# A mixture-of-experts layer that computes, for each token, only the two experts it chose

## The reference

```
scores = sigmoid(xf @ Wg.T + bg + bias)                 # 8 experts
top_scores, top_idx = top_k(scores, 2)
weights = zeros(T, 8).at[arange(T), top_idx].add(top_scores)
h  = gelu(einsum('td,ehd->teh', xf, W1) + b1)           # hidden width 512
eo = einsum('teh,edh->ted', h, W2) + b2
combined = einsum('ted,te->td', eo, weights)            # 6 of 8 weights are zero
shared = gelu(xf @ Ws1.T + bs1) @ Ws2.T + bs2
x = x + shared + combined
```

## Time and profile before

| | |
|---|---|
| median of 3 runs | 1903.09 us |
| the profiled execution's span, first to last instruction | 1898.6 us |
| the difference, what lies around the span | 4.5 us |
| the expert layer, first `up` to last `down` | 155.7 to 656.6 us |
| busy share of the span: PE, DVE, ACT, POOL | 91%, 55%, 71%, 13% |
| mean granted TensorE clock | 0.979 |

### The profile page before, as it was taken

The page is one execution under the profiler, slowest core; times in us unless marked ns, Lnnn a source line. Parts: engine busy times, 40 slices in busy tenths (PEclk is TensorE's granted clock), DMA queues, the critical chain, the costliest instruction groups (busy, mean ns, idle before and its releaser), DMA issues.

```text
span 1898.6 us, 47095 instructions
## 1 busy us (share of the span) xinstructions
PE 1727.9 (91%) x19832; PEld 1120.0 (59%) x19832; DVE 1041.5 (55%) x2670; ACT 1346.8 (71%) x1589; POOL 240.9 (13%) x160
## 2 busy tenths in 40 slices
PE   3458999999999989999999999999988899999998
PEld 2347999999997745555555555555544455555554
DVE  6985212222224445555555555555547777777773
ACT  0454444444443489999999999999998577677765
POOL 6454000000000200000000000000000112211122
PEclk9768999999999999999999999999999999999999
DMA  8001000000000333333333333333230000000000
GB/s 290 1 1 48 1 1 1 1 1 1 1 1 1 65 85 84 86 86 85 86 82 84 84 84 84 80 83 79 58 104 4 1 7 6 6 6 1 7 7 12
DMA packets 36213, 85.68 MB, mean 45 GB/s; under 512 B 10649, under 2 KB 23330, under 8 KB 35618
## 3 DMA queue, kind: packets, MB, share of 16 engines
q1 hardware_dynamic: 33954, 76.30, 17.0%
q0 software_dynamic: 2048, 6.36, 1.1%
HBM read 30.43 MB, written 2.10 MB: 17 GB/s over the span
## 4 chain that ended last, share of the span: by engine, by line
PE 45%; issue 38%; DVE 5%; POOL 2%; ACT 2%; POOLq 0%; ACTq 0%; DVEq 0%
PE C_ps_s L692 14%; PE C_ps_s L679 11%; PE C_ps_s L1149 6%; PE C_ps_s L1158 6%; PE C_ps_o L1174 2%; PE C_ps_p L1139 2%; POOL C_o_t L1942 1%; DVE D_gated L1377 1%; PE C_ps_o L1799 1%; PE C_ps_s L697 1%; ACT D_hidden L1237 1%; DVE C_den_t L2068 1%; ACT C_probs L1904 0%; PE C_ps_p L1134 0%; PE C_ps_s L1784 0%
## 5 line engine op out<-in xcount | busy, mean ns | idle before, releaser
L1904 ACT ACTIVATE C_probs<-C_ps_s 128x1024 f32<-128x1024 f32 x832 | 771.6, 1064 | 30.8 <-PE C_ps_s L1784 30.5
L1799 PE MATMUL C_ps_o<-C_probs,C_values 128*16 128x256 f32 x6656 | 440.6, 382 | 7.9 <-DVE C_o_t L2064 7.3
L1237 ACT ACTIVATE D_hidden<-C_ps_s,D_b_up 128x1024 f32<-128x1024 f32 x256 | 275.4, 1114 | 133.2 <-PE C_ps_s L1149 133.0
L753 ACT ACTIVATE B_hidden<-C_ps_s,B_b_up 128x512 f32<-128x512 f32 x288 | 192.0, 689 | 196.0 <-PE C_ps_s L679 195.4
L692 PEld LDWEIGHTS C_ps_s<-B_w_down,B_hidden 128*128 128x128 f32 x2304 | 269.8, 192 | 10.4 <-ACT B_hidden L753 1.2
L692 PE MATMUL C_ps_s<-B_w_down,B_hidden 128*128 128x128 f32 x2304 | 275.9, 276 | 0.0
L1799 PEld LDWEIGHTS C_ps_o<-C_probs,C_values 128*16 128x16 f32 x6656 | 154.3, 96 | 146.7 <-ACT C_probs L1904 10.3
L1784 PE MATMUL C_ps_s<-C_queries,C_keys 32*128 32x256 f32 x3328 | 211.8, 328 | 26.2 <-ACT C_probs L1904 25.0
L1784 PEld LDWEIGHTS C_ps_s<-C_queries,C_keys 32*128 32x128 f32 x3328 | 127.0, 183 | 154.8 <-ACT C_probs L1904 115.0
L856 DVE SCALAR_TENSOR_TENSOR B_acc<-C_ps_s,B_gate,B_acc 128x128 f32<-128x128 f32 x224 | 63.1, 344 | 273.5 <-PE C_ps_s L692 273.5
L1149 PE MATMUL C_ps_s<-D_up_in,D_w_up_r 128*128 128x512 f32 x512 | 185.4, 443 | 1.8 <-ACT D_hidden L1237 1.8
(11 more groups left out here) (275 smaller groups left out, 1961.8 us busy)
## 6 DMA issues: line engine op xcount, KB each, us to landing
C_keys<-C_k_hi SPq DMA_DIRECT2D x128, 200.1 KB, 4.3
C_ctx_t<-ctx_t_dram SPq DMA_DIRECT2D x16, 800.5 KB, 4.4
C_keys<-C_k_lo SPq DMA_DIRECT2D x64, 200.1 KB, 4.1
C_queries<-C_q_hi SPq DMA_DIRECT2D x128, 32.0 KB, 2.3
B_w_up<-L_ffn_w_up_dram SPq DMA_DIRECT2D x1, 2304.0 KB
B_w_down<-L_ffn_w_down_dram SPq DMA_DIRECT2D x1, 2304.0 KB, 20.0
C_queries<-C_q_lo SPq DMA_DIRECT2D x64, 32.0 KB, 2.3
C_queries<-C_blank SPq DMA_DIRECT2D x16, 128.0 KB, 2.6
```

The lines of the kernel that those rows point to most:

```text
L753: nc.scalar.activation(hidden[:, e % HB, c, :], ps_h[c][:], ACT.Gelu, bias=b_up[:, u:u + 1]).then_inc(s_hid, 1)
L1237: nc.scalar.activation(hidden[:, u % RING, :, :], ps_u[u % 2][:], ACT.Gelu, bias=b_up[:, u % PAIRS:u % PAIRS + 1]).then_inc(s_hid, 1)
L1799: m = T.matmul(ps_o[32 * j:32 * j + 2 * DK, g % 2, :], values[:, parity, kt, g * HG + j, :], probs[:, slot(parity, 2 * step + j // 2), j % ...
L1904: nc.scalar.activation(probs[:, slot(parity, n)], ps_s[bank(k, n)][:], ACT.Exp, scale=SCORE_SCALE1).then_inc(s_exp, 1)
```

## The change

The subject is cut in a dense and a sparse part. The shared expert stays dense: 8 blocks of 512 tokens, `up_shared` and `down_shared`, the result added straight into `x_sb`. For the 8 chosen-by-score experts, the 4096 tokens are cut in two parts of 2048. For each part the kernel counts the tokens per expert, gives every (token, choice) a row in a list sorted by expert whose runs are padded to multiples of 256 rows, and GpSimd scatters the normalised rows by indirect DMA into an HBM buffer (`sorted_rows`, zeroed beforehand by SP). The list has 23 units of 256 rows per part, whatever the data, so 46 in all. One unit belongs to one expert; its number is read from a table in SBUF into a register by VectorE and by ScalarE, and the weights are fetched from the resident arrays at that register's address: VectorE splits them in high and low part (`w_hi`, `w_lo`), ScalarE copies the down weights (`w_dn`). TensorE transposes the unit's rows, runs `up` and `down` over 256 rows, VectorE adds the bias, and SP stores the result to a second HBM buffer. Later GpSimd gathers the two result rows of each token (`gather`), and VectorE multiplies them by their scores and adds them to `x_sb` (`combine`): for the first 8 tiles beside the units, for the rest inside the batches of the head attention. The preparation of the head attention's first batch moves beside the units 8 to 41.

```
+PARTS0, UNIT = 2, 256
+UNITS0 = (2 * TOKENS // PARTS0 + EXPERTS0 * (UNIT - 1)) // UNIT     # 23
+NV = PARTS0 * UNITS0                                                # 46
...
     # SP, end of the first layer
+                sp.wait_ge(s_window[BLOCKS - 1], 16 * BT)
+                loads_after.clear(sp)
...
     # SP, the units
+        def load(v):
+            if v in (0, UNITS0):
+                sp.wait_ge(s_sent[v // UNITS0], 16 * 2 * TP)
+            wait(sp, s_ut, v - 3)
+            sp.dma_start(unit_in[:, v % 4], rows_of(sorted_rows, v)).then_inc(s_in[v % 4], 16)
+        def store(v):
+            sp.wait_ge(s_y, v + 1)
+            sp.dma_start(rows_of(result_rows, v), unit_out[:, v % 2]).then_inc(s_ys[v % 2], 16)
+        for v in range(3):
+            load(v)
+        for v in range(NV):
+            if v + 3 < NV:
+                load(v + 3)
+            if v > 0:
+                store(v - 1)
+            beside(v)
...
     # TensorE
+        def down_shared(k):
+            pe.wait_ge(s_hid, CH * (k + 1))
...
+            for i in range(BT):
                 for c in range(CH):
+                    T.matmul(ps_e[k % 2][:, i, :], hidden_s[:, (k + 1) % 2, c, i * P:(i + 1) * P],
+                             w_down[:, SHARED, c, :], start=(c == 0), stop=False)
+                m = T.matmul(ps_e[k % 2][:, i, :], ones[0:1, :], b_down[0:1, SHARED, :], start=False, stop=True)
...
+        def up(v):
+            pe.wait_ge(s_us, v + 1)
+            pe.wait_ge(s_uw, v + 1)
+            for c in range(CH):
+                if c % 2 == 0:
+                    pe.wait_ge(s_hid, gelus_to(v - 1) if v > 1 else CH * BLOCKS - 2 + 2 * v)
+                for n, (w, x) in enumerate(((w_hi, unit_hi), (w_hi, unit_lo), (w_lo, unit_hi))):
+                    m = T.matmul(ps_s[v % 2][:, c // 2, c % 2, :], w[:, v % 2, c * P:(c + 1) * P], x[:, v % 2, :],
+                                 start=(n == 0), stop=(n == 2))
...
+        def down(v):
+            pe.wait_ge(s_hid, gelus_to(v + 1))
+            pe.wait_ge(s_wd, v + 1)
+            wait(pe, s_y, v - 1)
+            if v + 2 < NV:
+                pe.wait_ge(s_us, v + 3)
+            for i in range(2):
+                for c in range(CH):
+                    m = T.matmul(ps_s[2][:, v % 2, 1, i * D:(i + 1) * D], hidden[:, (v + 2) % 3, c, i * P:(i + 1) * P],
+                                 w_dn[:, v % 2, c, :], start=(c == 0), stop=(c == CH - 1))
...
+        for k in range(BLOCKS):
+            up_shared(k)
+            if k in (1, 7):
+                ranks(k // 7)
...
+            if k > 0:
+                down_shared(k - 1)
...
+        for v in range(NV):
+            if v == 0:
+                up(0)
+                down_shared(BLOCKS - 1)
+                turn_unit(1)
+                continue
+            if v + 1 < NV:
+                turn_unit(v + 1)
+            up(v)
+            down(v - 1)
+            beside(v)
...
     # ScalarE
+        def gelus(v):
+            act.wait_ge(s_tables, 1 + v // UNITS0)
+            e = act.value_load(expert[0:1, v:v + 1], min_val=0, max_val=GROUPS0 - 1)
+            if v > 1:
+                act.wait_ge(s_down, downs_to(v - 1))
+            A.copy(w_dn[:, v % 2].rearrange("p c d -> p (c d)"),
+                   w_down[:, bass.ds(e, 1)].rearrange("p e c d -> p (e c d)")).then_inc(s_wd, 1)
...
+            for c in range(CH):
+                if c % 2 == 0:
+                    act.wait_ge(s_up, ups_to(v) + c // 2 + 1)
+                A.activation(hidden[:, (v + 2) % 3, c, :], ps_s[v % 2][:, c // 2, c % 2, :], ACT.Gelu,
+                             bias=b_unit[:, v % 4, c:c + 1]).then_inc(s_hid, 1)
...
     # GpSimd
+    def scatter(pool, p):
+        if p == 0:
+            pool.wait_ge(loads.s_cleared, 16 * PARTS0)
+        pool.wait_ge(s_slots, p + 1)
+        pool.wait_ge(s_xn, TP * (p + 1))
+        for t in range(p * TP, (p + 1) * TP):
+            for n in range(2):
+                nc.gpsimd.indirect_dma_start(
+                    sorted_rows[p], bass.IndirectOffsetOnAxis(slots[:, n, t:t + 1], axis=0),
+                    rows_n[:, t, :], None).then_inc(s_sent[p], 16)
...
     # VectorE
+        def prepare(v):
+            if v % UNITS0 == 0:
+                dve.wait_ge(s_tables, 1 + v // UNITS0)
+            e = held[v % 3] = dve.value_load(expert[0:1, v:v + 1], min_val=0, max_val=GROUPS0 - 1)
+            if v > 1:
+                dve.wait_ge(s_up, ups_to(v - 1))
+            weights = w_up[:, bass.ds(e, 1), :].rearrange("p e h -> p (e h)")
+            chain.mark(V.tensor_copy(w_hi[:, v % 2], weights))
+            chain.mark(V.tensor_copy(b_unit[:, v % 4], b_up[:, bass.ds(e * CH, CH)]))
+            dve.wait_ge(s_ut, v + 1)
+            rows = ps_s[2][:, v % 2, 0, :]
+            chain.mark(V.tensor_copy(unit_hi[:, v % 2], rows))
+            chain.settle()
+            V.tensor_tensor(unit_lo[:, v % 2], rows, unit_hi[:, v % 2].bitcast(F32), ALU.subtract).then_inc(s_us, 1)
+            V.tensor_tensor(w_lo[:, v % 2], weights, w_hi[:, v % 2].bitcast(F32), ALU.subtract).then_inc(s_uw, 1)
+        def finish(v):
+            e = held[v % 3]
+            dve.wait_ge(s_down, downs_to(v + 1))
+            wait(dve, s_ys[v % 2], 16 * (v // 2))
+            V.tensor_tensor(unit_out[:, v % 2], ps_s[2][:, v % 2, 1, :].rearrange("p (i d) -> p i d", d=D),
+                            b_down[:, bass.ds(e, 1), :].to_broadcast([P, 2, D]), ALU.add).then_inc(s_y, 1)
...
+        for v in range(NV):
+            if v + 1 < NV:
+                prepare(v + 1)
+            if v > 0:
+                finish(v - 1)
+                beside(v)
...
     # where the first batch's preparation and the combining lie
+        FIRST_AT = {**{8 + i: i for i in range(len(KEY_AT))}, 31: 7, 32: 8, 33: 9, 34: 10, 35: BEFORE_SCORES}
+        COMBINE_FIRST_AT = {29: 0, 38: 1}
+        STATISTICS_FIRST_AT = {30: 0, 39: 1}
+        COMBINE_AT, COMBINED_STATISTICS_AT = 15, 17
...
     # GpSimd in the second block
+                pool.wait_ge(sparse.s_down, sparse.downs)
                 empty_values(0)
```

More of the change, by code:

```diff
@@ L622, in expert_layer @@
[L622 to L630, removed]
+    E = EXPERTS0
+    SHARED = EXPERTS0
+    TP = TILES // PARTS0
+    HALF = [P, TP, E]
+    shared_hi = over["keys0"]("shared_hi", [P, 4, BT, P], F32R)
@@ L672, in logits @@
             lg.then_inc(s_logit, 1)
-        def up(k, parity, e):
-            for c in range(CH):
[L676 to L680, removed]
-                                         start=(n == 0), stop=(n == 2))
-                m.then_inc(s_up, 1)
@@ new lines, in gather @@
+    def gather(pool, j):
+        p = j // (TILES // (BT * PARTS0))
+        units = UNITS0 * (p + 1)
+        for i in range(2):
+            pool.wait_ge(s_ys[i], 16 * ((units + 1 - i) // 2))
+        wait(pool, s_combined, BT * j)
+        for i in range(BT):
+            for n in range(2):
+                nc.gpsimd.indirect_dma_start(
+                    gathered[:, i, n, :], None, result_rows[p],
+                    bass.IndirectOffsetOnAxis(slots[:, n, BT * j + i:BT * j + i + 1], axis=0)).then_inc(s_yg, 16)
@@ new lines, in on_vector @@
+        split_w8()
+        scores(0)
+        split_shared(2)
+        split_shared(3)
+        choose(0)
+        normalize(4)
+        assign(0)
+        tabulate(0)
+        normalize(5)
+        add_shared(0)
+        normalize(6)
+        split_shared(4)
+        normalize(7)
+        add_shared(1)
+        split_shared(5)
+        add_shared(2)
+        split_shared(6)
+        add_shared(3)
+        split_shared(7)
+        add_shared(4)
+        scores(1)
+        choose(1)
+        add_shared(5)
@@ new lines, in on_vector @@
+        assign(1)
+        tabulate(1)
+        add_shared(6)
+        prepare(0)
+        add_shared(7)
+        for v in range(NV):
+            if v + 1 < NV:
[3 more added lines that the diff above has]
+                beside(v)
+        return lambda: finish(NV - 1)
+    return SparseExperts(on_sync, on_tensor, on_scalar, on_vector, scatter, gather, combine, s_down, s_hid, s_y, s_ut,
+                         s_tables, s_ys, downs_to(NV), gelus_to(NV))
@@ L1647, in _ @@
             def _(sp):
-                loads.start(sp)
                 def move_sums(b, parity):
@@ L1922, in _ @@
                 pool.sem_inc(s_blank, 1)
+                for j in range(2):
+                    sparse.gather(pool, j)
                 def empty_values(parity):
@@ L1943, in multiply @@
                                         ALU.mult).then_inc(s_divided, 1)
-                with pool.Fori(0, BATCH // 2) as i:
-                    multiply(2 * i, 0)
-                    multiply(2 * i + 1, 1)
+                for b in range(BATCH):
+                    multiply(b, b % 2)
+                    if b % 2 == 1 and 3 <= (b + 5) // 2 < TILES // BT:
+                        sparse.gather(pool, (b + 5) // 2)
                 experts.on_gpsimd(pool)
```

617 lines of the change are left out of this document (375 added, 242 removed).

## The result

The changed kernel takes **1751.1 us** (median of 4 runs, 1747.45 to 1754.14) against 1903.8 for the kernel before in the same series; the ratio of the times is 0.9195, 95% interval 0.9184 to 0.9206. 1747 had been forecast, with 1692 to 1825 around it. The profiled execution took 1747.45 us; its span is 1745.6.

The account below looks back on a forecast made before the run. TensorE bounded the expert layer (498.6 of 500.9 us busy). First weighted sum at 256 + 206 + 34 + 4 = 500 instead of 661.4, 161 us earlier, less 5: 156 off 1903.1 gives 1747 us, range 1692 to 1825.

Parts of the forecast that it names:

- the closed chain: Units: each `down` waits through `finish`, register read, casts and subtraction on VectorE for the next, 4.6 us per unit (3.9 to 5.5).
- The first `up`: Start of the shared expert: VectorE's extra cast, subtraction and three blocks to normalise delay it by 2.5 us.
- The shared expert: Eight dense blocks of 8.8 us each, 70.3 us, with some 9 us of transposes, scoring and ranking between them.
- The way into the units: TensorE idles through two preparations of about 4 us each, with `up`s and the first `down` between: 14 us.
- One unit: Sparse units: from one `down` to the next 4.56 us, say 4.6, bounds 3.9 and 5.5.
- the register read: VectorE's read of the unit's expert number, with `finish` running under it: 1.1 us in the chain, 0.42 to 2.0.
- the rival with 3.9 and 1715: Units: VectorE's sequencer reads ahead, hiding the register read; 3.9 us per unit, 1715 us in all; chance 0.2.
- The jobs: First head-attention batch's preparation on VectorE, between `finish` and the next register read: 34 us added, bounds 20 and 50.
- Scatter and gather: GpSimd starts an indirect DMA every 1.25 us; the first 32 scatters cost nothing, with 20 us of cover.
- the rival of starved descriptors: GpSimd's scatters held up by VectorE casts, 5.85 us each; 1924 us, slower than before; chance 0.05.
- Half clock: Rival: TensorE falls to 1.2 GHz in the units, making the chain 6.3 us and the time 1822; chance 0.13.
- The end: After the last `down`: 4.3 us to the first weighted sum; combining and statistics add 5 us to the head attention.

## Why the prediction was right, and where two errors met

The forecast named the bound of the new stage, the closed chain, and that step held. Its legs, forecast and measured in the profiled execution (us):

| leg | forecast | measured |
|---|---|---|
| start to first `up` | 158.2 | 162.0 |
| first `up` to the end of the first unit's `down` | 97.8 | 93.0 |
| to the end of the last `down` | 240 | 234.9 |
| to the first weighted sum | 4.3 | 5.7 |
| from there to the end, with what lies around the span | 1246.7 | 1251.9 |
| sum | 1747 | 1747.5 |

The sum is closer than its terms deserve, and that is luck: 9.9 us too much in two legs, 10.4 too little in three. The lower end of the range does not follow from what it names: a free register read (45 x 0.7) and 20 us of jobs instead of 34 give 1701, not 1692.

- *The first `up`*: forecast 2.5 us later than before, measured 6.3. What I left out is that the logits of two blocks now stand directly ahead of it. VectorE has the first block's operands ready at 157.25; TensorE is still at its transposes and logits until 162.04:

```profile
156.56 0.69 DVE L1001 TENSOR_TENSOR B_w_lo<-B_w_up,B_w_hi 128x512 fp32r<-128x512 f32 x1
```
```profile
158.77 3.42 PE L787 MATMUL C_ps_o<-B_w_gate,B_xt 128*128 128x8 f32 x16
162.04 0.77 PE L813 MATMUL C_ps_s<-B_shared_hi,B_w_hi 128*128 128x512 f32 x1
```

  The last 16 logits take 3.42 us, 0.21 each. TensorE had been busy for 3.4 of the 11 us before 151, and from there to the first `up` it has the lower of its clocks (1.2 GHz), as the window shows:

```profile
151.00:162.00 11.00, 10.10 (x48) 9.76 (x49) 6.15 (x18) 3.63 (x5) 0.00 (x0) 0.50 0.63 210
```

  This reason rests on the trace alone.
- *The shared expert*: the blocks' 8.8 us and the transposes between them held (`add_shared` every 10.04 to 10.08 us where a transposed block lies between), and so did 0.42 for the one-row bias matmul. The way into the units took some 12 us where 14 were forecast. The rest of the 4.8 lies before it: blocks, passes between them, slow start and choice took 81.0 us together, where 83.6 had been forecast.
- *One unit*: 4.37 instead of 4.56. `down` 2.02 (1.95 forecast); `finish` and read 0.76 (1.1); the weights' cast and the bias copy 0.42 (0.41); the rows' cast 0.45 (0.42), their subtraction 0.42; hops 0.30 (0.25). The mis-sized term is the register read. A read was 0.75 us in the median of the earlier trace rows; here it is 0.30:

```profile
L1069 DVEq TENSOR_LOAD <-B_expert x46: 300/304/739, 236.6 to 479.9; - x46
L1069 DVEq FUSED_REGOPS  x46: 190/190/204, 237.2 to 480.2; - x46
```

  The shortest read of before (305 ns) is the ordinary one here; what made those in the earlier trace rows longer no run shows. As a price in the chain it is 0.42, between "free" (the rival with 3.9 and 1715) and the 0.7 that I charged.
- *The jobs*: 34 us forecast, 34.7 measured, as the intervals' sum of 234.9 less 43 x 4.37, the last two (3.19 and 2.43) and the stall. A key job costs 1.0, the combines and statistics 4 to 5 each.
- *What no step had*: GpSimd's memset, 6.65 us. The prediction priced the values' memset and not the keys'.
- *Scatter and gather*: 970 ns each and one every 1.27 us (POOL's line, ns min/median/max), as the earlier trace rows had it for gathers alone, and landing in 2.2 us:

```profile
L949 POOL DMA_INDIRECT B_sorted_rows<-B_rows_n,B_slots x64: 965/970/1486, 174.6 to 274.1; - x64
```

  The longest is 1.49 us, so the rival of starved descriptors (5.85 us each) is refuted. Nor is there a wait like the example (620 to 3100 ns) of the Trainium skill, SBUF — State Buffer, section "SBUF: two separate sides", that the prediction weighed against the change. A small hindrance is there: the two long ones of the 64 each start 0.03 to 0.04 us behind VectorE's subtraction of the low weights, and so do those of 1.48 to 1.49 us in nine of the ten other kernels.

```profile
252.61 0.68 DVE L1080 TENSOR_TENSOR B_w_lo<-B_w_up,B_w_hi 128x512 fp32r<-128x512 f32 x1
```
```profile
252.65 1.49 POOL L949 DMA_INDIRECT B_sorted_rows<-B_rows_n,B_slots  x1 [0.30 <-issue]
```

  It costs 0.5 us each time and lies off the chain.
- *Half clock*: 0.94 over the units and 1.00 at 350 to 400 us, where only plain units run. The rival is refuted for the plain unit; behind stalls the lower clock is real (`down` of 3.64 us).
- *The end*: 5 us forecast, 10.2 measured. The head attention takes 6.4 more (the combines and their statistics 6.1 of it, as above); the start is 2.8 better (26.1 instead of 28.9 us from the first weighted sum to the first copy of the sums); the last layer's span is 9.2 us longer, of which 2.65 come back as less time around the span. In the later runs 1.8 us lie around the span (2.0 in one), of the kernel before too, so the 4.5 that I had used probably held some 2.7 us by which that profiled execution was faster than the median. Of the 9.2 us some 5 lie behind the last addition, 8.1 instead of 2.9 us to the end of the span: SP's last wait there, 5.4 us (0.2 before), is for TensorE's sequencer, and why that is late no run shows; it is there in every kernel here that has the change. The other 4 go with the last layer's lower clock (0.98 instead of 1.00).

The median, 1751.1, is 3.6 above the profiled execution. The four runs' mean clocks are 0.963, 0.958, 0.957 and 0.956 for 1747.5, 1750.9, 1751.3 and 1754.1 us. That the clock drops behind stalls is shown; that these drops make the whole difference is not, since filling one idle stretch raised the mean clock and left the median where it was.

## What to carry to other kernels

When work is cut to a fraction, look for the closed chain through two engines before adding up busy times: here one shared PSUM bank cost 0.95 us in each plain unit, and one wait moved to another place was worth 49 us after the arithmetic had been cut. A price inside such a chain (a register read, 0.42 us) is worth its full size, and nothing once the chain is open, so open the chain first. And a long instruction of an idle engine is not free: look at what it shares with the engine that is in the chain.

## What the runs showed of the hardware that I had not expected

- A VectorE copy of 128 x 4 elements lasted 5.49 us beside a GpSimd MEMSET of 5.71; of eight MEMSETs of 0.77 us, the seven that fell into VectorE's waits held nothing up.
- An indirect DMA of 128 rows, 0.97 us on GpSimd, lasted 1.48 to 1.49 where it started 0.03 to 0.04 us behind a VectorE subtraction of two SBUF tensors (0.68 us), with one exception (0.96).
- A register read on VectorE, 0.30 us and 0.19 of arithmetic on it, starts only when the instructions ahead of it are issued; ahead of the wait for `down` it was hidden, behind it it cost 0.42 us.
- TensorE starts an independent matmul while the last pass of the one before is under way: 3.42 us from unit to unit, though `down` alone lasts 1.95 us from its first start to its last end and adds only 1.78.
- The wait view can name an instruction that ended at the right moment and has nothing to do with the wait; it took the code and two runs to see that ScalarE was not in the chain.
